# A mixture-of-experts kernel: the exponentials of the fourth routing batch on VectorE as a series instead of ScalarE's table

## The chip, the cores and the metric

The kernel runs on one core of a Trainium2 chip. The metric is the device time of one execution in microseconds (us), as a median over runs. The engines are TensorE (PE in the rows, its weight loads PEld), VectorE (DVE), ScalarE (ACT), GpSimd (POOL) and the DMA queues, which SyncE (SP) and GpSimd start.

## The reference

Input are 8 sequences of 512 rows with 128 features. First comes an LSTM over the 8 sequences (the step runs over the first axis), then a layer norm of x + LSTM(x). Its rows are split into 8 groups of 512 tokens and go through a layer of 8 experts, each token to its best two, with a capacity of 128 tokens for each pair of group and expert. A second layer norm closes.

```python
raw = jax.nn.softmax(logits, axis=-1)          # logits = x @ router_w, 8 experts
idx1 = jnp.argmax(raw, axis=-1)
gate1 = jnp.sum(raw * one_hot(idx1), axis=-1)
rest = raw * (1.0 - one_hot(idx1))
idx2 = jnp.argmax(rest, axis=-1)
gate2 = jnp.sum(rest * one_hot(idx2), axis=-1)
# places in an expert's queue by a cumulative sum, tokens past the capacity are dropped
hidden = gelu(expert_in @ w0) * (expert_in @ w1)
out = combine(hidden @ wo, gate1, gate2)
```

## The kernel before, in words

**First part, the LSTM (0 to about 64 us of the trace).** A loop over the sequences s = 0 to 7 computes the gates with TensorE, activates them on ScalarE (tanh), combines them on VectorE. Among these steps stand the layer norm and the router of the sequences that are done. The router works in four batches b of two groups (8 tiles of 128 tokens each). For a batch, `best` (L938) takes the top values of the logits and writes their distance from the largest into `less`; `scale_less` (L950) multiplies it by the reciprocal deviation; `exp` (L745) on ScalarE writes `ex`, the exponentials, 128 partitions by 64 values; the five steps of `gate_step` (L958) on VectorE sum, divide and choose; `assign_batch` computes each token's slot; GpSimd's `scatter` writes the rows into the experts' slots in DRAM, 16 indirect transfers per batch (L479). The scatters of the four batches stand one behind the other in GpSimd's queue.

**Second part, the experts.** 24 units u, each one expert with two or four groups of slots, are run in a written order. SyncE loads a unit's rows (`load_xd`, L407, into `xd`) once the batches that feed it are scattered. TensorE turns them (`turn_xd`, L594, into `b_xt`), ScalarE and VectorE split the turned rows into a high and a low half (`x_hi` L791, `x_lo` L1082). A unit has 6 chunks k = 0 to 5. For each chunk TensorE computes two products in `first` (L645 to L647, three matmuls each, from the high and low halves of rows and weights; the last chunk has one product). ScalarE applies the gelu (L834, tile `act_g`), VectorE multiplies by the second product (`chunk`, L1116, into one of four buffers called `term_f`, `term_i`, `cell`, `h`), ScalarE makes the high half of the result (L797, `hid_hi` or `h_hi`), VectorE the low half one chunk later (L1090, `hid_lo` or `h_lo`), and TensorE uses both in `second` (L661, L662, L664; for the last chunk L667, L668), three chunks behind `first`. After a unit its output is turned (`turn_y`, L681) and `give` (L1106, L1108) weights it and hands it to GpSimd, which adds it into the tokens in DRAM (L494).

**Around the change.** The first exponential of this part belongs to batch 2 and stands ahead of unit 0. The exponential of the last batch (NB - 1 = 3) stands on ScalarE in unit 1, chunk 4, after the copy of unit 0's output (L803) and the high half of unit 2's rows (L791) and ahead of the gelu of that chunk. The function table that ScalarE holds at that point has the gelu, so the compiled program loads another for the exponential and the gelu's again after it (two `ACT_TABLE_LOAD`). On VectorE `scale_less(3)` stands after chunk 2 of unit 1 and the first step of `gate_step(3)`, which reads `ex`, after chunk 0 of unit 2. The engines' programs run in the order in which they are written; an instruction that waits for a semaphore holds all behind it on its engine.

```python
elif (u, k) == (1, 4):            # ScalarE
    exp(NB - 1)
...
scale_less(NB - 1)                # VectorE
low_weights(2, 3)
for k in range(3, NCH):
    chunk(1, k)
for k in range(NCH):
    chunk(2, k)
    if k < 3:
        for n in range(2 * k, min(2 * k + 2, 5)):
            gate_step(NB - 1, n)
```

## Time and profile before

| | |
|---|---|
| runs, us | 346.48, 347.69, 651.17; median 347.69 |
| profiled execution, its own time | only its span is given |
| span of the profiled execution, us | 342.1 |
| median less span, us | 5.6 |
| busy, share of the span | TensorE 86%, VectorE 74%, ScalarE 64%, GpSimd 55% |
| instructions in the span | 5646 |

The span runs from the first to the last instruction of one execution; a run's time has the start and the end around it. The profile's page gives each engine's busy time, slices of the span, and a chain of waits followed back from the end. A timeline lists instructions with their start, their duration, the engine, the line and the tiles, and in brackets how long the engine was idle before and what it waited for. TensorE's matmuls are pipelined: the starts of its records follow each other more closely than their durations, and the ends are modelled.

### The profile page before, as it was taken

To read this page: it belongs to the slowest core of one execution; us is meant where nothing else is said; L and a number is where in the kernel's file an instruction comes from. 1 tells how busy PE (TensorE), PEld (TensorE's weight loads), DVE (VectorE), ACT (ScalarE), POOL (GpSimd) and SP (SyncE) were. 2 spreads that over 40 slices of the span, in tenths; PEclk is the share of its full clock that TensorE was granted. 3 is DMA by queue.
4 is the path that set the end of the run, shared out by engine and by line. 5 is a ranking of instruction groups with operands and counts; after the bars stand their busy time and mean duration, and the time that the engine had idled before them with its cause. 6 is when DMAs were issued, how large, how long until landed. Compare 5 with 4: busy or idle time off the path is not lost.

```text
span 342.1 us, 5646 instructions
## 1 busy us (share of the span) xinstructions
PE 293.1 (86%) x1692; PEld 244.8 (72%) x1692; DVE 251.6 (74%) x794; ACT 217.3 (64%) x495; POOL 186.6 (55%) x153
## 2 busy tenths in 40 slices
PE   8999999697754695529999999999999999998880
PEld 6666665496744695419999987877888888888770
DVE  2789989599621585026888889889877776996985
ACT  4689887665720473026777876877765566566884
POOL 5012788887777027787773433437436536559500
PEclk9999999999885598557999999999999999999996
DMA  6996582486521015324443326344214227325265
GB/s 218 363 407 167 127 251 74 99 229 191 166 89 57 22 28 151 97 35 47 49 62 57 52 46 175 76 113 64 47 16 63 33 19 134 65 36 86 24 163 153
DMA packets 46685, 37.20 MB, mean 109 GB/s; under 512 B 7057, under 2 KB 40784, under 8 KB 46656
## 3 DMA queue, kind: packets, MB, share of 16 engines
q1 hardware_dynamic: 35392, 26.56, 26.1%
q0 software_dynamic: 11264, 10.29, 19.6%
q8 instruction: 14, 0.23, 0.3%
q14 instruction: 15, 0.12, 0.1%
HBM read 17.86 MB, written 17.10 MB: 102 GB/s over the span
## 4 chain that ended last, share of the span: by engine, by line
PE 67%; DVE 10%; issue 7%; ACT 6%; another core or an unknown queue 5%; POOL 3%; DMA 1%; SPq 0%; ACTq 0%; DVEq 0%
PE big L647 11%; PE big L645 11%; PE big L646 10%; PE big L552 6%; PE b_ht L664 3%; PE b_xnt L661 2%; PE b_xnt L664 2%; PE b_xnt L662 2%; PE b_ht L661 2%; PE b_ht L662 2%; PE big L538 2%; POOL tokens L494 2%; PE b_rt L681 2%; PE big L539 2%
## 5 line engine op out<-in xcount | busy, mean ns | idle before, releaser
L834 ACT ACTIVATE act_g<-big 128x256 f32<-128x256 f32 (+1 forms) x144 | 65.0, 452 | 90.8 <-PE big L647 59.6
L645 PE MATMUL big<-x_hi,e_hi 128*128 128x256 f32 (+1 forms) x264 | 89.5, 339 | 0.3 <-issue 0.3
L647 PE MATMUL big<-x_lo,e_hi 128*128 128x256 f32 (+1 forms) x264 | 86.9, 329 | 1.3 <-issue 1.3
L646 PE MATMUL big<-x_hi,e_lo 128*128 128x256 f32 (+1 forms) x264 | 86.9, 329 | 1.0 <-issue 1.0
L479 POOL DMA_INDIRECT slots<-rows,slot_ix x64 | 68.5, 1071 | 33.6 <-issue 18.5
L494 POOL DMA_INDIRECT tokens<-contrib,token_ix x32 | 51.4, 1607 | 42.2 <-DVE token_ix L1108 34.4
L494 POOL DMA_INDIRECT tokens<-zero_rows,token_ix x28 | 45.2, 1614 | 35.5 <-DVE token_ix L1108 27.5
L646 PEld LDWEIGHTS big<-x_hi,e_lo 128*128 128x128 f32 x264 | 52.9, 200 | 4.5 <-issue 1.1
L647 PEld LDWEIGHTS big<-x_lo,e_hi 128*128 128x128 f32 x264 | 52.7, 199 | 4.4 <-issue 0.4
L645 PEld LDWEIGHTS big<-x_hi,e_hi 128*128 128x128 f32 x264 | 53.0, 201 | 3.7 <-issue 0.2
L1116 DVE TENSOR_TENSOR term_i<-act_g,big 128x256 f32<-128x256 f32 (+3 forms) x36 | 18.3, 508 | 17.4 <-ACT act_g L834 12.0
L1116 DVE TENSOR_TENSOR term_f<-act_g,big 128x256 f32<-128x256 f32 (+1 forms) x36 | 18.3, 508 | 17.2 <-remote 12.9
L1116 DVE TENSOR_TENSOR cell<-act_g,big 128x256 f32<-128x256 f32 (+1 forms) x36 | 18.3, 509 | 14.1 <-ACT act_g L834 8.9
L1116 DVE TENSOR_TENSOR h<-act_g,big 128x256 f32<-128x256 f32 (+3 forms) x36 | 18.3, 508 | 13.6 <-PE big L647 6.5
L762 ACT ACTIVATE act_g<-big,bias_g 128x512 f32<-128x512 f32 x31 | 21.2, 687 | 9.0 <-PE big L552 6.4
L552 PE MATMUL big<-h,u_half 128*128 128x512 f32 x56 | 25.5, 598 | 0.2 <-DVE h L1062 0.2
L460 POOL TENSOR_TENSOR root_y<-root_x,minus_half 128x4 f32<-128x4 f32 x8 | 9.7, 1216 | 25.5 <-DVE root_x L929 25.5
L661 PE MATMUL b_xnt<-hid_hi,e_hi 128*128 128x256 f32 (+1 forms) x48 | 17.2, 358 | 3.7 <-ACT hid_hi L797 1.9
L738 ACT ACTIVATE e_hi<-e_raw 128x544 fp32r<-128x544 f32 x32 | 20.4, 650 | 0.0
L661 PE MATMUL b_ht<-hid_hi,e_hi 128*128 128x256 f32 (+1 forms) x48 | 16.8, 349 | 3.0 <-issue 1.7
L797 ACT ACTIVATE hid_hi<-cell 128x256 fp32r<-128x256 f32 (+1 forms) x36 | 17.3, 482 | 2.9 <-DVE cell L1116 2.1
L664 PE MATMUL b_ht<-hid_lo,e_hi 128*128 128x256 f32 (+1 forms) x48 | 16.5, 344 | 3.1 <-DVE hid_lo L1090 2.0
(204 smaller groups left out, 672.9 us busy)
## 6 DMA issues: line engine op xcount, KB each, us to landing
e_raw<-in_L_ffn_w_kernel_dram SPq DMA_DIRECT2D x16, 320.0 KB
slots<-zero_rows SPq DMA_DIRECT2D x8, 548.0 KB, 7.6
e_raw<-in_L_ffn_wo_kernel_dram SPq DMA_DIRECT2D x8, 320.0 KB
xd<-slots SPq DMA_DIRECT2D x16, 137.0 KB
xd<-slots SPq DMA_DIRECT2D x8, 274.0 KB
e_lo<-e_raw POOLq DMA_DIRECT2D x4, 544.0 KB
x<-in_L_attn_input_seq_dram SPq DMA_DIRECT2D x8, 256.0 KB, 4.5
tokens<-rows SPq DMA_DIRECT2D x8, 256.0 KB
```

The costliest lines, as they stand in the source:

```text
L479: pool.indirect_dma_start(slots, bass.IndirectOffsetOnAxis(ap=slot_ix[b][:, 2 * t + c:2 * t + c + 1], axis=0), rows[:, b * BT + t, :], Non ...
L494: pool.indirect_dma_start(tokens, bass.IndirectOffsetOnAxis(ap=tokens_of(u)[:, k:k + 1], axis=0), contrib(u)[:, k, :], None, bounds_check= ...
L552: pe.matmul(big[k][:, :], u_half[:, g * D:(g + 1) * D], h2[:, :], start=False, stop=True).then_inc(gate_ready, 1)
L645: pe.matmul(dst, e_hi[q][:, c0:c0 + m], xdt_hi[u % 2][:, 0:w], start=True, stop=False)
L646: pe.matmul(dst, e_lo[q][:, c0:c0 + m], xdt_hi[u % 2][:, 0:w], start=False, stop=False)
L647: mm = pe.matmul(dst, e_hi[q][:, c0:c0 + m], xdt_lo[u % 2][:, 0:w], start=False, stop=True)
L661: pe.matmul(y, hi, hid_hi[r][:, 0:w], start=(k == 0), stop=False)
L664: mm = pe.matmul(y, hi, hid_lo[r][:, 0:w], start=False, stop=False)
L738: nc.scalar.activation(e_hi[e % RING_E][:, piece(n)], e_raw[e % 2][:, piece(n)], ACT.Copy).then_inc(ehi_ready[e % RING_E], 1)
L762: nc.scalar.activation(act_g[k][:, :], big[k][:, :], ACT.Tanh, bias=bias_g[:, gate_order[k]:gate_order[k] + 1], scale=1.0 if k == 2 else 0 ...
L834: nc.scalar.activation(act0[n % RH][0:m, 0:w], pre(n, P)[0], ACT.Gelu_apprx_tanh).then_inc(gelu_ready, 1)
L1116: dve.tensor_tensor(hid[n % RH][0:m, 0:w], act0[n % RH][0:m, 0:w], pre(n, P)[1], ALU.mult).then_inc(hid_ready, 1)
```

## The change

The call of `exp` for the last batch leaves ScalarE. In its place VectorE computes the same 128 by 64 exponentials in 14 steps (15 instructions), all in float32: the argument is cut off at -87, divided by ln 2 and rounded (by adding and taking away 1.5 * 2^23), the rest is formed with ln 2 in two parts, the power of two is put together as an integer, and a polynomial of degree seven is evaluated by Horner's rule; values under -87 become 0. Each step but one instruction waits for the step before it by a semaphore of its own, `exp_step`. The steps stand ahead of the last three chunks of unit 1: four, five and five. Batches 0, 1 and 2 keep ScalarE's exponential. Five work tiles are added, 128 by 64 each.

```diff
--- before.py
+++ after.py
@@ -9,6 +9,7 @@
 
 
 
+import math
 from contextlib import ExitStack
 
 import concourse.bass as bass
@@ -70,6 +71,11 @@
     AS = 6
     RH = 4
 
+    SERIES = [1.0 / math.factorial(n) for n in range(7, 0, -1)]
+    EXP_STEPS = 7 + len(SERIES)
+    EXP_LOW, LOG2E, ROUND = -87.0, 1.4426950408889634, 1.5 * (1 << 23)
+    LN2_HIGH, LN2_LOW = 0.693359375, -2.12194440054690e-4
+
     gate_order = [1, 0, 3, 2]
 
     with ExitStack() as ctx:
@@ -130,6 +136,9 @@
         top_ix = sb("top_ix", [P, BT, E], U32)
         less, ex = sb("less", [P, BT, E]), sb("ex", [P, BT, E])
         total, rtotal = sb("total", [P, BT]), sb("rtotal", [P, BT])
+        ex_x, ex_n = sb("ex_x", [P, BT * E]), sb("ex_n", [P, BT * E])
+        ex_r, ex_q = sb("ex_r", [P, BT * E]), sb("ex_q", [P, BT * E])
+        ex_two = sb("ex_two", [P, BT * E], I32)
         gates = sb("gates", [P, BT, 2])
         choice = sb("choice", [P, BT, 2])
         chosen = sb("chosen", [P, BT, 2, E], BF16)
@@ -197,6 +206,7 @@
         var_ready, power_ready, root_ready = sem("var_ready"), sem("power_ready"), sem("root_ready")
         xn_ready = sem("xn_ready")
         logits_ready, scaled, exp_ready = sem("logits_ready"), sem("scaled"), sem("exp_ready")
+        exp_step = sem("exp_step")
         top_ready, less_ready, topix_ready, gates_step = sem("top_ready"), sem("less_ready"), sem("topix_ready"), sem("gates_step")
         base_step = sem("base_step")
         chosen_ready, places_ready, slot_step = sem("chosen_ready"), sem("places_ready"), sem("slot_step")
@@ -822,8 +832,6 @@
                         norm_rows(S - 2, range((k - 1) * T // 2, k * T // 2))
                     elif (u, k) in ((0, 4), (0, 5)):
                         norm_rows(S - 1, range((k - 4) * T // 2, (k - 3) * T // 2))
-                    elif (u, k) == (1, 4):
-                        exp(NB - 1)
                     n = u * NCH + k
                     m = P if k < FULL else P // 2
                     if n >= RH:
@@ -954,6 +962,35 @@
                 dve.wait_ge(power_ready, GB * (b + 1))
                 view = less[:, :, :].rearrange("p (g t) e -> p g t e", g=GB)
                 dve.tensor_tensor(view, view, root_y[:, :, 0:T].unsqueeze(3).broadcast_to([P, GB, T, E]), ALU.mult).then_inc(scaled, 1)
+
+            def exp_by_series(n):
+
+                x, out = less[:, :, :].rearrange("p t e -> p (t e)"), ex[:, :, :].rearrange("p t e -> p (t e)")
+                if n:
+                    dve.wait_ge(exp_step, n)
+                else:
+                    dve.wait_ge(scaled, NB)
+                if n == 0:
+                    ins = dve.tensor_scalar(ex_x[:, :], x, EXP_LOW, None, ALU.max)
+                elif n == 1:
+                    ins = dve.tensor_scalar(ex_n[:, :], ex_x[:, :], LOG2E, ROUND, ALU.mult, ALU.add)
+                elif n == 2:
+                    ins = dve.tensor_scalar(ex_n[:, :], ex_n[:, :], -ROUND, None, ALU.add)
+                elif n == 3:
+                    ins = dve.scalar_tensor_tensor(out=ex_r[:, :], in0=ex_n[:, :], scalar=-LN2_HIGH, in1=ex_x[:, :], op0=ALU.mult, op1=ALU.add)
+                elif n == 4:
+                    dve.tensor_scalar(ex_two[:, :], ex_n[:, :], 127.0, float(1 << 23), ALU.add, ALU.mult)
+                    ins = dve.scalar_tensor_tensor(out=ex_r[:, :], in0=ex_n[:, :], scalar=-LN2_LOW, in1=ex_r[:, :], op0=ALU.mult, op1=ALU.add)
+                elif n == 5:
+                    ins = dve.tensor_scalar(ex_q[:, :], ex_r[:, :], SERIES[0], None, ALU.mult)
+                elif n < 5 + len(SERIES):
+                    ins = dve.scalar_tensor_tensor(out=ex_q[:, :], in0=ex_q[:, :], scalar=SERIES[n - 5], in1=ex_r[:, :], op0=ALU.add, op1=ALU.mult)
+                elif n == 5 + len(SERIES):
+                    ins = dve.scalar_tensor_tensor(out=ex_q[:, :], in0=ex_q[:, :], scalar=1.0, in1=ex_two[:, :].bitcast(F32), op0=ALU.add, op1=ALU.mult)
+                else:
+                    dve.scalar_tensor_tensor(out=out, in0=x, scalar=EXP_LOW, in1=ex_q[:, :], op0=ALU.is_ge, op1=ALU.mult).then_inc(exp_ready, 1)
+                    return
+                ins.then_inc(exp_step, 1)
 
             def gate_step(b, n):
 
@@ -1210,6 +1247,8 @@
             scale_less(NB - 1)
             low_weights(2, 3)
             for k in range(3, NCH):
+                for n in range(EXP_STEPS * (k - 3) // 3, EXP_STEPS * (k - 2) // 3):
+                    exp_by_series(n)
                 chunk(1, k)
             for k in range(NCH):
                 chunk(2, k)
```

On ScalarE in unit 1, from the copy of unit 0's output on, before the change (`tanh_c` is the tile of that copy, `act_g` the gelu's output, `hid_hi<-term_i` the high half of chunk 3):

```order
L803 ACTIVATE tanh_c<-b_ht 128x256
L791 ACTIVATE x_hi<-b_xt 128x256
L747 ACT_TABLE_LOAD
L747 ACTIVATE ex<-less 128x64
L834 ACT_TABLE_LOAD
L834 ACTIVATE act_g<-big 128x256
L797 ACTIVATE hid_hi<-term_i 128x256
```

and after it:

```order
L813 ACTIVATE tanh_c<-b_ht 128x256
L801 ACTIVATE x_hi<-b_xt 128x256
L842 ACTIVATE act_g<-big 128x256
L807 ACTIVATE hid_hi<-term_i 128x256
L842 ACTIVATE act_g<-big 64x256
```

The two table loads and the exponential are gone; the gelu of chunk 4 follows the high half of unit 2's rows directly.

On VectorE in unit 1, from the low half of a piece of expert 2's weights (`e_lo`) over chunks 3 and 4 up to chunk 5 (`term_i`, `cell` and `h` are the outputs of chunks 3, 4 and 5, `x_lo` the low half of unit 2's rows), before the change:

```order
L1027 TENSOR_TENSOR e_lo<-e_raw,e_hi 128x544
L1116 TENSOR_TENSOR term_i<-act_g,big 128x256
L1090 TENSOR_TENSOR hid_lo<-term_f,hid_hi 128x256
L1082 TENSOR_TENSOR x_lo<-b_xt,x_hi 128x256
L1116 TENSOR_TENSOR cell<-act_g,big 128x256
L1090 TENSOR_TENSOR hid_lo<-term_i,hid_hi 128x256
L1116 TENSOR_TENSOR h<-act_g,big 64x256
```

and after it, up to the last step ahead of chunk 4:

```order
L1064 TENSOR_TENSOR e_lo<-e_raw,e_hi 128x544
L974 TENSOR_SCALAR ex_x<-less 128x64
L976 TENSOR_SCALAR ex_n<-ex_x 128x64
L978 TENSOR_SCALAR ex_n<-ex_n 128x64
L980 SCALAR_TENSOR_TENSOR ex_r<-ex_n,ex_x 128x64
L1153 TENSOR_TENSOR term_i<-act_g,big 128x256
L1127 TENSOR_TENSOR hid_lo<-term_f,hid_hi 128x256
L1119 TENSOR_TENSOR x_lo<-b_xt,x_hi 128x256
L982 TENSOR_SCALAR ex_two<-ex_n 128x64
L983 SCALAR_TENSOR_TENSOR ex_r<-ex_n,ex_r 128x64
L985 TENSOR_SCALAR ex_q<-ex_r 128x64
L987 SCALAR_TENSOR_TENSOR ex_q<-ex_q,ex_r 128x64 x3
```

Four instructions of the series came in ahead of chunk 3 and of everything behind it, `x_lo` among it, and six ahead of chunk 4.

On VectorE from chunk 4 of unit 1 on, after the change:

```order
L1153 TENSOR_TENSOR cell<-act_g,big 128x256
L1127 TENSOR_TENSOR hid_lo<-term_i,hid_hi 128x256
L987 SCALAR_TENSOR_TENSOR ex_q<-ex_q,ex_r 128x64 x3
L989 SCALAR_TENSOR_TENSOR ex_q<-ex_q,ex_two 128x64
L991 SCALAR_TENSOR_TENSOR ex<-less,ex_q 128x64
L1153 TENSOR_TENSOR h<-act_g,big 64x256
```

Five more instructions came in ahead of chunk 5. No instruction of TensorE, GpSimd or SyncE moved.

## Rows read from the trace of the kernel before

**Rows 1.** The page, part 1: busy time of each engine.
```profile
PE 293.1 (86%) x1692; PEld 244.8 (72%) x1692; DVE 251.6 (74%) x794; ACT 217.3 (64%) x495; POOL 186.6 (55%) x153
```

**Rows 2.** Stretches: length, busy us (instructions) per engine, granted clock, DMA, GB/s.
```profile
88.00:92.00 4.00, 2.19 (x11) 1.98 (x10) 2.17 (x7) 3.30 (x8) 3.19 (x3) 0.77 0.81 259
92.00:96.00 4.00, 3.56 (x25) 3.36 (x24) 2.03 (x8) 0.88 (x3) 3.09 (x4) 0.81 0.43 123
96.00:118.00 22.00, 11.12 (x57) 9.36 (x57) 6.58 (x25) 5.56 (x17) 11.86 (x13) 0.60 0.15 47
130.00:155.00 25.00, 10.52 (x52) 9.00 (x51) 5.70 (x15) 4.48 (x14) 19.27 (x18) 0.59 0.41 95
155.00:180.00 25.00, 25.00 (x202) 25.00 (x202) 20.80 (x58) 17.37 (x53) 18.52 (x12) 0.93 0.43 53
```

**Rows 3.** Timeline of TensorE: start, us, engine, line, op, tiles, idle before.
```profile
86.92 0.28 PE L664 MATMUL b_xnt<-hid_lo,e_hi 128*128 128x256 f32 x1
...
87.08 0.41 PE L681 MATMUL b_xt<-ident,tanh_c 128*128 128x128 f32 x2
...
88.01 0.28 PE L647 MATMUL big<-x_lo,e_hi 128*128 128x256 f32 x1
...
90.09 0.57 PE L661 MATMUL b_xnt<-hid_hi,e_hi 128*128 128x256 f32 x1 [1.81 <-issue]
...
94.72 0.28 PE L647 MATMUL big<-x_lo,e_hi 128*128 128x256 f32 x1
...
95.44 0.44 PE L594 MATMUL b_xt<-ident,xd 128*128 128x128 f32 x2 [0.44 <-DMA xd<-slots]
...
95.95 0.29 PE L664 MATMUL b_ht<-hid_lo,e_hi 128*128 128x256 f32 x1
```

**Rows 4.** Timeline of ScalarE around the fourth exponential.
```profile
86.49 1.28 ACT L747 ACT_TABLE_LOAD   x1
87.78 0.26 ACT L747 ACTIVATE ex<-less 128x64 f32<-128x64 f32 x1
88.06 1.28 ACT L834 ACT_TABLE_LOAD   x1
89.35 0.38 ACT L834 ACTIVATE act_g<-big 128x256 f32<-128x256 f32 x1
89.63 0.41 ACT L797 ACTIVATE hid_hi<-term_i 128x256 fp32r<-128x256 f32 x1
```

**Rows 5.** Timeline of VectorE in the same stretch.
```profile
85.67 0.42 DVE L1116 TENSOR_TENSOR term_i<-act_g,big 128x256 f32<-128x256 f32 x1
...
86.51 0.43 DVE L1082 TENSOR_TENSOR x_lo<-b_xt,x_hi 128x256 fp32r<-128x256 f32 x1
...
89.77 0.42 DVE L1116 TENSOR_TENSOR cell<-act_g,big 128x256 f32<-128x256 f32 x1 [2.84 <-ACT act_g L834]
...
90.11 0.42 DVE L1090 TENSOR_TENSOR hid_lo<-term_i,hid_hi 128x256 fp32r<-128x256 f32 x1
...
90.56 0.42 DVE L1116 TENSOR_TENSOR h<-act_g,big 64x256 f32<-64x256 f32 x1
...
93.57 0.42 DVE L1090 TENSOR_TENSOR hid_lo<-term_f,hid_hi 128x256 fp32r<-128x256 f32 x1
```

**Rows 6.** Groups of VectorE by form: busy us, mean ns.
```profile
L956 DVE TENSOR_TENSOR less<-less,root_y 128x64 f32<-128x64 f32 x4 | 0.9, 219 | 0.0
```

**Rows 7.** Timeline of VectorE, two dependent steps of an earlier batch's softmax.
```profile
31.22 0.20 DVE L966 RECIPROCAL rtotal<-total 128x8 f32<-128x8 f32 x1
31.45 0.17 DVE L969 TENSOR_TENSOR gates<-ex,rtotal 128x16 f32<-128x16 f32 x1
```

**Rows 8.** Timeline of GpSimd's queue, the last scatter of batch 1.
```profile
89.48 0.98 POOL L479 DMA_INDIRECT slots<-rows,slot_ix  x1 [0.30 <-issue]
```

**Rows 9.** Timeline of SyncE's queue, the loads of unit inputs behind it.
```profile
92.97 38.19 SPq L407 DMA_DIRECT2D xd<-slots  x5
```

**Rows 10.** Timeline of ScalarE after 95 us.
```profile
108.66 0.38 ACT L834 ACTIVATE act_g<-big 128x256 f32<-128x256 f32 x1 [6.78 <-remote]
```

## The prediction, made before the changed kernel ran

> **What bounds the kernel now.** I read the busy times first: TensorE is busy 293.1 us of 342.1, more than any other engine [rows 1], so ScalarE's time counts only where TensorE waits for it. The windows then show where TensorE is not full: it is busy 2.19 us of the 4 from 88 to 92, 11.12 of 22 from 96 to 118 and 10.52 of 25 from 130 to 155, and full from 155 to 180 [rows 2]. The first of these holes lies on the edit. TensorE's timeline shows a matmul at 88.01 and the next at 90.09, the first of chunk 3's second product; where TensorE is full a matmul follows the one before it in 25 / 202 = 0.12 us [rows 2], so 2.08 less 0.12 = 1.96 us are lost [rows 3]. The bracket says only "issue", but ScalarE's timeline gives the cause: table load at 86.49, exponential at 87.78, table load at 88.06, gelu at 89.35, and only then, at 89.63, the high half of chunk 3, done at 90.04 [rows 4]. The granted clock of 88 to 92 is 0.77 and of 92 to 96 is 0.81 [rows 2]: together (0.23 + 0.19) x 4 x 2 = 3.4 us at the lower level, 1.2 GHz, right behind that wait; work that takes 3.4 us there takes 1.7 at 2.4 GHz. So the wait costs 2.0 us and up to 1.7 more.
>
> The question is what comes next. At 95.44 TensorE turns the rows of unit 3, after waiting 0.44 us for the DMA that brings them [rows 3]. Its last matmul ahead of that starts at 94.72 and ends at 95.00, so the rows were there at about 95.4, and TensorE was early. These rows are group 2 and 3's slots: SyncE issues their load at 92.97 [rows 9], once batch 1's scatter has landed, whose last issue starts on GpSimd at 89.48 in a queue that has idled only 0.30 us between issues [rows 8]. Neither queue has an instruction that the edit moves, and this scatter waits for nothing that ScalarE or VectorE do in unit 1.
>
> **ScalarE's side.** Removed: 1.28 + 0.26 + 1.28 us and the small gaps between, 86.49 to 89.35 = 2.86 us [rows 4]. Without it the gelu of chunk 4 starts at 86.49, the high half of chunk 3 at 86.77 and is done at 87.18, before TensorE asks for it at 88.13 or later. The wait for ScalarE is gone entirely; what is late next is VectorE.
>
> A rule of the Trainium skill says more: "ScalarE: Activation LUTs", section "What ACT_TABLE_LOAD costs", puts a switch at 1283 ns for the load and about 1380 ns for a drain. By that two switches would cost 5.3 us, and the edit would free 5.6 us of ScalarE. The trace agrees with the load (1.28) and shows no drain: both loads, the exponential and all gaps fit into 2.86 us [rows 4]. I go by the trace.
>
> **VectorE's side.** 15 instructions of 128x64 float32 come in. The nearest form is `scale_less`, also 128x64: 219 ns [rows 6]. From one dependent step to the next there is little: the reciprocal starts at 31.22, takes 0.20, and the step that waits for it by a semaphore starts at 31.45, 0.03 later [rows 7]. So 0.25 us for a dependent step; one of the 15 doesn't wait for the one before and costs about 0.14. The sum is 14 x 0.25 + 0.14 = 3.6 us: 1.0 ahead of chunk 3, 1.4 ahead of chunk 4, 1.25 ahead of chunk 5. The 0.14 is the 0.22 less an overlap of 0.08, which instructions that don't wait for each other show: one at 89.77 takes 0.42, the next starts at 90.11 [rows 5]. Bounds for a step: 0.14 for every step would make 2.1 us for all; 0.42, what an instruction with four times as many elements takes [rows 5], would make 6.3. I take 0.25, since the form is the same as that of [rows 6].
>
> Walked through: chunk 3 starts at 85.67 + 1.0 = 86.7 and `x_lo`, two instructions of 0.34 later, at 87.35, done at 87.8 where it was done at 86.94 [rows 5]. The turning of unit 0's output waits for it and moves from 87.08 to about 87.85; the products of unit 2's chunk 0 behind it, whose last matmul starts 0.93 later at 88.01 [rows 3], are started by 88.8 instead of 88.0, and TensorE is free at 88.9. The second batch of steps ends at 89.1; chunk 4, which waited for the gelu until 89.77 [rows 5], starts then, and chunk 3's low half is done at 89.9. TensorE needs it for the third matmul from there, at 89.15, so it waits 0.75 us where it waited 2.0. The third batch of steps ends at 91.0, where chunk 5 starts, 0.5 later than its 90.56. From there to the end of the instruction at 93.57 VectorE ran without a longer break in 3.4 us [rows 5]; now it is done at 94.4 and not 94.0. In all VectorE, which had idled 2.84 us ahead of 89.77 [rows 5], fills that gap with the series and comes out 0.4 us later. The instruction at 93.57 makes the low half that TensorE uses at 95.95 [rows 3]: slack of 1.5 us left. TensorE itself, held twice by VectorE (low halves of chunks 4 and 5), comes to the turning of unit 3 at about 94.2, 0.8 us before it did, and then waits for the same DMA until 95.44.
>
> **Sum.** Saved up to 95 us: 2.0 of waiting and up to 1.7 of clock, less about 2.9 us of new waits for VectorE's low halves, in all 0.8. Given back at 95.44: 0.8. From there every engine has the same work in the same order, with three instructions fewer on ScalarE, long past; the first reader of `ex` on VectorE stands behind unit 2's chunk 0, the series is done before chunk 5 of unit 1, by 91.0, so the routing of batch 3 isn't later. The span stays at 342.1 less at most a few tenths. With the 5.6 us around it (median 347.69 less span 342.1) that is 347.7; I take 0.4 off, for what a warmer clock at 95 may give, and say 347.3.
>
> **Rivals.** (a) The gain is carried on. For it: from 96 on the engines wait for things that the trace doesn't name (ScalarE is idle 6.78 us ahead of the gelu at 108.66, "remote" [rows 10]); if TensorE's results already come late at 95, the edge at 95.44 is softer than it reads, and work ahead of it counts. Against it: the bracket names the DMA. Time: at most 2.0 + 1.7 = 3.7 us off, 344.0.
>
> (b) The hole of 96 to 118 belongs to the first. It holds 57 matmuls in 22 us, and 155 to 180 holds 202 in 25 [rows 2]; at that rate 57 take 7.1, so 15 us are lost there, and I can't name what holds the results. If TensorE's pause of 2 us and its lowered clock set it off, it goes with them: 347.7 - 15 - 2 = 331. Against it: the like hole of 130 to 155 has no table load ahead of it.
>
> (c) VectorE becomes the bound and the kernel is slower. From the numbers above a step may cost 1.5 / 15 = 0.10 us more, 0.35, before the low half for 95.95 is late. At 0.6 us a step, if the semaphore's round trip or the conversion to an integer costs so much, it is 15 x 0.25 = 3.75 late, with a pause that keeps the clock low for 3.4 us more (1.7): 353.1.
>
> (d) The two long holes are sensitive to small shifts and one more appears or one grows: 15 us, 363.
>
> (e) The edit doesn't do what it says: the compiled order shows no table load left in unit 1, so I give this nothing.
>
> **How the numbers follow.** Forecast 0.62, (a) 0.17, (b) 0.09, (c) 0.08, (d) 0.04. The forecast's own range is 346 to 348.5, the spread of the undisturbed runs shown. For 8 in 10 the range takes in (a), nearly all of (c), and some growth or shrinkage of the holes by a third; (b) and (d) stay out: 341.5 to 351.5. A change of over 2% (7 us) is about what a measurement of this kernel can tell from none. Faster by that: (b) and a part of a shrinking hole, 0.10. Slower: (d) and a tail of (c), 0.06. Within: 0.84.
>
> **What would show it.** Right: no table load between 86 and 90, ScalarE's gelu of chunk 4 near 86.5; VectorE busy through 87 to 90 with 15 instructions at 0.25 us; no gap of TensorE over 1 us before 95; the turning of unit 3 again at about 95.4, now after a longer wait for the DMA (over 1 us); the span within 1 us. Wrong: that turning clearly before 95 or with no wait, which is (a); 96 to 118 with over 100 matmuls, which is (b); steps of over 0.35 us and the low half behind 96, which is (c).

## The result, and the profile after

Changed kernel: median 348.82 us of 20 runs (345.26 to 707.34). Kernel before, beside it on the same chip: median 347.19 us of 20 runs (345.30 to 651.17). The ratio on record is 1.0098, 95% interval [1.0056, 1.0139]: 1% slower, where the forecast was 0.1% faster. A ratio is formed from each kernel's fast runs, those within 1.5% of its fastest, and so needn't be the quotient of the medians beside it, which are of all runs. The 1.0098 can't be rebuilt from the 20 runs of each kernel: the medians give 1.0047, and the means without the three runs over 400 us give 1.0035, give or take 0.0042, which doesn't exclude 1.

One thing is needed to read all that follows: the runs went to several chips. The first comparison ran at a level of about 348 us, as chip 11 has it later; on three other chips (15, 3 and 1) the kernel before takes 306 us, with the same instructions. I call them the slower chip and the faster chips.

The page of the kernel after, its span and part 1:

```profile
span 348.5 us, 5658 instructions
PE 293.6 (84%) x1692; PEld 245.2 (70%) x1692; DVE 254.3 (73%) x809; ACT 215.0 (62%) x492; POOL 185.7 (53%) x153
```

Against [rows 1]: VectorE has 15 instructions and 2.7 us more, ScalarE three instructions and 2.3 us less, TensorE nearly the same. The run of this profile took 350.68 us, so 2.2 us lie around the span. I had set 5.6 for it, because for the kernel before I had only its span and the median of other runs. Its profiled run lay at 342.1 + 2.2 = 344.3 us, below every run listed for it: an unusually fast one.

The windows after, in the stretches of [rows 2] (without 118 to 130) and two ahead of them (length, busy us and instructions of TensorE, its weight loads, VectorE, ScalarE and GpSimd, granted clock, DMA share, GB/s):

```profile
80.00:84.00 4.00, 2.90 (x21) 2.50 (x21) 3.90 (x21) 1.05 (x3) 3.08 (x4) 1.00 1.02 306
84.00:88.00 4.00, 1.44 (x9) 1.26 (x8) 0.85 (x3) 0.68 (x2) 3.08 (x4) 0.72 0.20 67
88.00:92.00 4.00, 2.77 (x14) 2.39 (x13) 0.76 (x2) 0.69 (x2) 3.08 (x4) 0.50 0.19 63
92.00:96.00 4.00, 2.76 (x11) 2.17 (x10) 2.24 (x8) 0.69 (x2) 3.08 (x4) 0.50 0.19 46
96.00:118.00 22.00, 6.31 (x26) 5.75 (x27) 5.68 (x22) 3.67 (x12) 11.69 (x12) 0.50 0.30 94
130.00:155.00 25.00, 14.31 (x97) 12.86 (x95) 10.41 (x31) 7.95 (x23) 16.97 (x17) 0.78 0.35 99
155.00:180.00 25.00, 21.21 (x158) 20.91 (x159) 17.22 (x48) 14.96 (x45) 20.09 (x14) 0.81 0.42 48
```

The slow stretch that began at about 94 us before begins at about 81 us after: from 84 to 88 TensorE has 9 matmuls where the kernel before had 35:

```profile
84.00:88.00 4.00, 4.00 (x35) 3.88 (x34) 2.85 (x8) 3.17 (x8) 3.29 (x3) 1.00 0.40 110
```

ScalarE's gelus show what an engine sees inside the stretch:

```profile
80.65 0.38 ACT L842 ACTIVATE act_g<-big 64x256 f32<-64x256 f32 x1 [0.39 <-PE big L657]
...
85.65 0.38 ACT L842 ACTIVATE act_g<-big 128x256 f32<-128x256 f32 x1 [4.04 <-PE big L657]
...
89.96 0.38 ACT L842 ACTIVATE act_g<-big 128x256 f32<-128x256 f32 x1 [3.62 <-PE big L657]
...
113.96 0.38 ACT L842 ACTIVATE act_g<-big 128x256 f32<-128x256 f32 x1 [10.20 <-remote]
...
114.54 0.36 ACT L842 ACTIVATE act_g<-big 64x256 f32<-64x256 f32 x1
...
115.15 0.37 ACT L842 ACTIVATE act_g<-big 128x256 f32<-128x256 f32 x1
```

The gelus start 3 to 13 us apart and wait for TensorE's product, though TensorE itself is idle 5.0 of the 12 us from 84 to 96 (12 less 1.44, 2.77 and 2.76): the products reach the others late. The gelu at 85.65 starts 1.1 us behind the modelled end of its product's last matmul (84.25 + 0.28), the one at 89.96 starts 0.8 behind; in a trace of the same kernel on a faster chip each gelu from 85 to 112 us that waited for TensorE starts 0.1 behind. The gelu at 85.65 belongs to unit 1's chunk 0, three chunks ahead of the first series step. So in this profile the stretch begins ahead of the edit, and it can't be the edit's work that sets it off. The series' own steps stand at 94.70 and later here, among instructions that wait for the stretch. The prediction's signs can't be read in this profile: the gelu of unit 1's chunk 4, forecast for 86.5, is the one at 113.96, and unit 3's rows are turned at 120.2.

The stretch ends at the same time in both traces, at about 114 us, but with less done. The gelu at 115.15 is unit 2's first; the kernel before has unit 3's first there:

```profile
114.89 0.36 ACT L834 ACTIVATE act_g<-big 128x256 f32<-128x256 f32 x1
```

The changed kernel is one unit behind, and it stays so: unit 7's first gelu starts at 170.1 and not at 163.8, 6.3 us later, as much as the next unit takes in either trace. The spans differ by 6.4 us.

### The profile page after: what moved, and what is told of

Its sections match the earlier page's. It is cut to its first block, busy times and chain, and to the rows that moved or that the text cites. A ratio compares the mean times of both kernels' runs of the same rounds, so it can differ in the third digit from the quotient of the medians.

```text
span 348.5 us, 5658 instructions
## 1 busy us (share of the span) xinstructions
PE 293.6 (84%) x1692; PEld 245.2 (70%) x1692; DVE 254.3 (73%) x809; ACT 215.0 (62%) x492; POOL 185.7 (53%) x153
## 4 chain that ended last, share of the span: by engine, by line
PE 68%; issue 10%; DVE 9%; another core or an unknown queue 5%; ACT 5%; POOL 3%; ACTq 0%; DVEq 0%; POOLq 0%
PE big L657 11%; PE big L655 10%; PE big L656 10%; PE big L562 6%; PE b_ht L674 3%; PE b_xnt L671 3%; PE b_xnt L674 2%; PE b_xnt L672 2%; PE b_ht L671 2%; PE b_ht L672 2%; PE big L548 2%; POOL tokens L504 2%; PE b_rt L691 2%; PE big L550 2%
## 5 line engine op out<-in xcount | busy, mean ns | idle before, releaser
L489 POOL DMA_INDIRECT slots<-rows,slot_ix x64 | 67.2, 1050 | 41.6 <-DVE slot_ix L1053 22.1
L671 PEld LDWEIGHTS b_xnt<-hid_hi,e_hi 128*128 128x128 f32 x48 | 9.9, 205 | 20.9 <-issue 11.4
L807 ACT ACTIVATE h_hi<-h 128x256 fp32r<-128x256 f32 (+3 forms) x36 | 17.4, 482 | 1.9 <-DVE h L1153 1.5
```

The source lines that it names most:

```text
L489: pool.indirect_dma_start(slots, bass.IndirectOffsetOnAxis(ap=slot_ix[b][:, 2 * t + c:2 * t + c + 1], axis=0), rows[:, b * BT + t, :], Non ...
L671: pe.matmul(y, hi, hid_hi[r][:, 0:w], start=(k == 0), stop=False)
```

## The experiments

Four theories. **A**: the series costs more than the table loads gave. **B**: the edit gives and takes nothing; where the late stretches begin decides the 1%, and that is chance. **C**: a longer pause of TensorE lowers its clock behind it, so a gain ahead of it is turned into a loss. **D**: batch 2's and 3's scatters hold TensorE's results back. Later **F**, the forecast's own step: what is gained ahead is given back at the turning of unit 3's rows. The runs came in five jobs, each with its own runs of the kernel before on the same chip; every ratio is to those.

### On the slower chip: unaltered, removed, both, placed behind

The first changes nothing. The second leaves out the fourth batch's exponential (its gates come from batch 2's), so it has neither table loads nor series:

```diff
-                    elif (u, k) == (1, 4):
-                        exp(NB - 1)
-                    dve.wait_ge(exp_ready, b + 1)
+                    dve.wait_ge(exp_ready, min(b, NB - 2) + 1)
```

The third is the changed kernel with ScalarE's exponential put back and the series written to a tile that nobody reads. The fourth puts each batch of series steps behind the chunk instead of ahead of it.

> The changed kernel once more, unaltered, for a second interval and a second trace. Theory A (the edit costs: VectorE's 15 instructions make TensorE late by more than the two table loads gave): again 1.005 to 1.014 of the kernel before. Theory B (nothing is lost or won by the edit, and what differs is how long the two stretches last in which TensorE's results come late, before unit 6): the ratio comes out at 1.000 to 1.005, and the trace has the stretches at other places or of other lengths than the first trace, with units 6 to 23 equal to the tenth of a us.

> The fourth exponential is left out on ScalarE and no series is put in: batch 3's gates are formed from the exponentials of batch 2, which still stand in ex. The removal alone. Theory A: the removal saves what it frees up to the wait for unit 3's rows, 0.990 to 0.998. Theory B and my forecast's step at 95.44: 0.998 to 1.002, since TensorE only comes earlier to a DMA that GpSimd's queue times. Theory C (the pause for the table loads is useful, because the late stretches follow dense work of TensorE): slower, 1.004 to 1.012, although work is only taken away.

> Both: ScalarE's exponential with its two table loads stays and gives the result, and VectorE computes the series beside it into a tile that nobody reads. The addition alone. Theory A: slower, 1.004 to 1.012. Theory B: 1.000 to 1.004, VectorE idles 2.8 us there anyway. Theory C: 0.998 to 1.003, since the pause is back.

> The changed kernel with each group of series steps behind its chunk instead of ahead of it, so that chunks 3, 4 and 5 of unit 1 and the low halves come 1.0 to 1.4 us earlier and only what follows them is held. Theory A (the low halves held by the series are the cost): most of the loss goes, 0.998 to 1.004. Theory B: as e1_again within 0.3%. Theory C: as e1_again or slower.

| | median us (runs) | lowest, highest | ratio, 95% interval |
|---|---|---|---|
| before | 349.36 (11) | 346.18, 353.10 | |
| unaltered | 348.46 (6) | 346.37, 351.02 | 1.0004 [0.9942, 1.0066] |
| removed | 345.48 (6) | 341.38, 348.86 | 0.9871 [0.9806, 0.9936] |
| both | 350.88 (6) | 345.47, 350.98 | 0.9963 [0.9874, 1.0053] |
| behind | 349.23 (6) | 345.97, 350.74 | 1.0013 [0.9956, 1.0070] |

The 1.0% didn't come back with the same kernel, though the two intervals overlap. The kernel with both costs says little: four of its six runs lie at 350.9 to 351.0, and only the other two enter its ratio, so its ratio is under 1 while its median is the highest of the five. The removal's 1.3% speaks for A, which had expected 0.2 to 1.0%. It was not measured alone on this chip again; on the faster chips below it comes out slower than before. The windows from 84 to 92 show what moves the time. Unaltered (span 348.8 us) and behind (span 343.8 us), with the same 15 steps:

```profile
84.00:88.00 4.00, 1.09 (x7) 0.88 (x7) 1.31 (x4) 0.68 (x2) 3.08 (x4) 1.00 0.21 69
88.00:92.00 4.00, 2.47 (x10) 2.10 (x10) 0.40 (x1) 0.00 (x0) 3.09 (x4) 0.56 0.15 51
```

```profile
84.00:88.00 4.00, 3.30 (x24) 2.69 (x23) 2.41 (x7) 1.74 (x7) 3.09 (x4) 1.00 0.20 69
88.00:92.00 4.00, 2.05 (x11) 1.45 (x11) 1.68 (x7) 0.60 (x3) 3.08 (x4) 1.00 0.71 202
```

In the first the stretch is there from 84, in the second from about 87. Unit 0's first gelu, ahead of all that the edit touches, starts at 74.9 in the first and at 72.0 in the second (73.7 in the profile after, 71.8 in that before). A late unit 0 doesn't bring an early stretch by itself, though: in two later traces of this chip, with the turning one chunk later (below), unit 0 starts at 73.1 (changed) and 74.6 (before), the stretch begins at about 88 and 90, and the spans are 345.6 and 344.6.

### On a faster chip: with more matmuls that keep TensorE warm

Meant for the slower chip, to see if a warmer clock at unit 0 sets where the stretch begins:

```diff
-            keep_warm(8, big[2])
+            keep_warm(16, big[2])
             turn_xd(0)
+            keep_warm(4, big[2])
```

for the kernel before, the changed one and the removal. The fourth, for D, lets batches 2 and 3 scatter only each token's first choice (half of their transfers; the second choice's rows are left out).

> The kernel before with 12 more idle matmuls around the turning of unit 0's rows (8 ahead of it, 4 behind), where TensorE waits 2 and 1 us. The traces so far fall into two kinds: in two of six TensorE's clock falls at 68 us, unit 0 starts its gelus at 73.7 or later instead of 71.8, and its results come late from 81 us on instead of 87 to 94; both have spans of 348.5 and 348.8 against 342 to 344. Theory B (the two kinds make the spread, whatever the edit): the high values near 350 get rare, 0.990 to 0.996 of the kernel before, and the trace has the clock at 1.0 from 60 to 85. If the kinds come from elsewhere: 0.998 to 1.006.

> The changed kernel with the same 12 idle matmuls, so that the edit is compared with less spread, against e5_warm_before. Theory A (the series costs more than the table loads): 0.5 to 1.4% above e5. Theory B (the edit moves nothing): within 0.4% of e5.

> The kernel before without the fourth exponential (batch 3's gates from the exponentials of batch 2) and with the same 12 idle matmuls: the removal alone, a second time. If e2_drop_exp's 0.987 is the removal's own gain: 0.8 to 1.5% below e5. If it was the draw of the runs: within 0.4% of e5. Theory C (the pause is useful): above e5.

> The kernel before, in which batches 2 and 3 scatter only the rows of the first choice: 8 transfers each in GpSimd's queue instead of 16, so 10.3 us less per batch; their second choices are left out of the result. The late results of TensorE ended in all six traces between 113 and 115 us, right behind the end of batch 2's scatter (last issue 109.4 to 110.5). Theory D (the scatters hold TensorE's results back, from some backlog on until they end): the first stretch ends near 103 and the second is some 10 us shorter, and the span falls by 10 to 20 us, 0.94 to 0.97. If the stretches don't hang on the scatters: they end where they did and the time is 0.995 to 1.005.

The kernel before took 306.12 us here (29 runs, 304.86 to 307.06), 41 us less, and no trace has a late stretch. Warmed before 306.56, 1.0043 [1.0015, 1.0072]; warmed after 307.30, 1.0033 [1.0010, 1.0056]; warmed removal 308.85, 1.0079 [1.0054, 1.0104]; half scatter 305.95, 0.9988 [0.9974, 1.0001]. So the edit is worth nothing here (1.0033 beside 1.0043), the removal alone costs 0.4% more than either, and D can't be tested where there is no stretch; the scatters bound nothing here. Why less work doesn't take less time shows in TensorE's timeline at the turning of unit 3's rows. Warmed before:

```profile
88.30 0.39 PE L662 MATMUL b_xnt<-hid_hi,e_hi 128*128 128x256 f32 x1 [1.69 <-ACT hid_hi L798]
...
93.12 0.28 PE L648 MATMUL big<-x_lo,e_hi 128*128 128x256 f32 x1
95.13 0.44 PE L594 MATMUL b_xt<-ident,xd 128*128 128x128 f32 x2 [1.73 <-DMA xd<-slots]
```

Warmed after:

```profile
86.46 0.39 PE L675 MATMUL b_xnt<-hid_lo,e_hi 128*128 128x256 f32 x1 [0.19 <-DVE hid_lo L1128]
...
88.81 0.38 PE L675 MATMUL b_xnt<-hid_lo,e_hi 128*128 128x256 f32 x1 [0.51 <-DVE hid_lo L1128]
...
90.77 0.39 PE L675 MATMUL b_xnt<-hid_lo,e_hi 128*128 128x256 f32 x1 [0.63 <-DVE hid_lo L1128]
...
92.16 0.36 PE L678 MATMUL b_xnt<-h_hi,e_lo 128*128 128x256 f32 x1 [0.30 <-DVE h_hi L1128]
...
93.07 0.28 PE L658 MATMUL big<-x_lo,e_hi 128*128 128x256 f32 x1
95.66 0.44 PE L604 MATMUL b_xt<-ident,xd 128*128 128x128 f32 x2 [2.32 <-DMA xd<-slots]
```

Warmed removal:

```profile
89.94 0.28 PE L648 MATMUL big<-x_lo,e_hi 128*128 128x256 f32 x1
96.08 0.69 PE L594 MATMUL b_xt<-ident,xd 128*128 128x128 f32 x2 [5.86 <-DMA xd<-slots]
```

One wait of 1.69 us for ScalarE is replaced by four for VectorE's low halves, 1.63 us in all, and all three end at the same DMA at 95 to 96 us, whenever they arrive. The removal arrives 3 us earlier and waits 5.86. The granted clock of 88 to 92 and of 92 to 96 is 0.68 and 0.89 in the warmed kernel before and 1.00 and 1.00 in the warmed changed one; in the removal it is 0.74 from 92 to 96 and 0.50 from 96 to 100.

### On another faster chip: plain, removed, filled, doubled

The changed kernel and the removal again without warming. The third puts matmuls of ones ahead of the wait, in the bank that the turning fills:

```diff
             def turn_xd(u):
+                if u == 3:
+                    pe.wait_ge(contrib_ready, 2 * min(u - 2, GB + 1))
+                    keep_warm(24, b_xd(u))
                 pe.wait_ge(xd_in[u % 4], 16 * (u // 4 + 1))
```

The fourth sets a further instruction of the same size ahead of each dependent step of the series:

```diff
-                    dve.wait_ge(exp_step, n)
+                    dve.wait_ge(exp_step, 2 * n)
...
+                dve.scalar_tensor_tensor(out=ex_s[:, :], in0=(ex_q if n > 5 else ex_x)[:, :] if n else x, scalar=1.0, in1=x, op0=ALU.add, op1=ALU.mult).then_inc(exp_step, 1)
+                dve.wait_ge(exp_step, 2 * n + 1)
```

> The changed kernel unaltered, once more. The two chips seen so far gave 349 and 306 us for the kernel before, and the long stretches in which TensorE's results come late stood only in the slower. The last three traces of the faster one show the edit at work: with the series TensorE waits 0.19, 0.51 and 0.63 us for low halves in unit 1 and 2, and comes to the turning of unit 3's rows at 93.3, where it waits 2.32 us for the DMA; without exponential and series it comes at 90.2 and waits 5.86. Theory F (the forecast: what is gained ahead is given back at this DMA): the time is that of before within 0.3%, on either chip: 306 +-1 at the faster. Theory A (the series costs more than the table loads gave): over 1.005, 308 or more. Theory B (the 1.0% measured belongs to the stretches of the slower chip, where a few tenths of a us decide how long they last): at the faster chip 1.000 +-0.003, at the slower anything within 1.5% of before.

> Leaves out the fourth batch's exponential altogether (the gates come from an older batch's, so the outputs differ), without the warming matmuls of the last run. Theory F with theory C (the pause is given back at the DMA, and a pause of over 5 us there lowers the clock of the 9 us that follow): 0 to 1% slower than before, 306 to 309 at the faster chip, with the granted clock under 0.8 right behind the turning of unit 3's rows. Theory A: 1% faster than before, 303. The difference to the changed kernel in the same job is the series' own price: under A +5 us, under F zero or below.

> As the run before it, and 24 matmuls of ones by ones are put ahead of TensorE's wait for unit 3's rows, into the bank that the turning then fills. They take 24 x 0.2 = some 5 us of a pause of 5.9 and delay nothing else. If the lowered clock behind that pause is what makes the removal slower (C), the time falls below that of the run without them by 1 to 3 us, to before's or just under (305 to 306 at the faster chip), and the granted clock stays at 1.00 from 92 to 106. If the pause's place and not the clock costs the time, it equals the run without them.

> The changed kernel with each dependent step of the series preceded by one more of the same size that writes to a tile that nobody reads and that the step waits for: 14 instructions more, 14 x 0.25 = 3.5 us more of VectorE ahead of chunks 3, 4 and 5 of unit 1. Theory A (the series stands on the path): the time grows by all of it, 3.5 us over the changed kernel. Theory F: the wait for unit 3's rows was 2.3 us at the faster chip and takes that much of it; the time grows by 3.5 - 2.3 = 1.2 us and up to 1 more by the clock, as TensorE's waits ahead of it grow to 1 us and more each. If it grows by nothing, the low halves of unit 2 have more slack than I read.

| | median us (runs) | ratio, 95% interval |
|---|---|---|
| before | 306.56 (23) | |
| changed, unaltered | 306.69 (12) | 1.0005 [0.9985, 1.0025] |
| removed | 308.35 (12) | 1.0050 [1.0022, 1.0077] |
| removed, filled with 24 | 308.25 (6) | 1.0058 [1.0037, 1.0080] |
| doubled | 310.80 (5) | 1.0133 [1.0112, 1.0154] |

The first agrees with the forecast's ratio (347.3 / 347.69 = 0.999) within 0.2%. VectorE's timeline of that run has the whole series (start, us, engine, line, op, tiles):

```profile
86.24 0.19 DVE L974 TENSOR_SCALAR ex_x<-less 128x64 f32<-128x64 f32 x1
86.46 0.20 DVE L976 TENSOR_SCALAR ex_n<-ex_x 128x64 f32<-128x64 f32 x1
86.69 0.20 DVE L978 TENSOR_SCALAR ex_n<-ex_n 128x64 f32<-128x64 f32 x1
86.92 0.23 DVE L980 SCALAR_TENSOR_TENSOR ex_r<-ex_n,ex_x 128x64 f32<-128x64 f32 x1
87.07 0.42 DVE L1153 TENSOR_TENSOR term_i<-act_g,big 128x256 f32<-128x256 f32 x1
...
88.06 0.19 DVE L982 TENSOR_SCALAR ex_two<-ex_n 128x64 int32<-128x64 f32 x1
88.16 0.22 DVE L983 SCALAR_TENSOR_TENSOR ex_r<-ex_n,ex_r 128x64 f32<-128x64 f32 x1
88.42 0.27 DVE L985 TENSOR_SCALAR ex_q<-ex_r 128x64 f32<-128x64 f32 x1
88.72 0.77 DVE L987 SCALAR_TENSOR_TENSOR ex_q<-ex_q,ex_r 128x64 f32<-128x64 f32 x3
89.41 0.41 DVE L1153 TENSOR_TENSOR cell<-act_g,big 128x256 f32<-128x256 f32 x1
...
90.07 0.73 DVE L987 SCALAR_TENSOR_TENSOR ex_q<-ex_q,ex_r 128x64 f32<-128x64 f32 x3
90.84 0.23 DVE L989 SCALAR_TENSOR_TENSOR ex_q<-ex_q,ex_two 128x64 f32<-128x64 f32 x1
91.10 0.23 DVE L991 SCALAR_TENSOR_TENSOR ex<-less,ex_q 128x64 f32<-128x64 f32 x1
91.36 0.42 DVE L1153 TENSOR_TENSOR h<-act_g,big 64x256 f32<-64x256 f32 x1
```

Dependent steps follow each other in 0.22 to 0.30 us, and the conversion to an integer (`ex_two`) is no dearer. The three batches take 87.07 - 86.24 = 0.83, 89.41 - 88.06 = 1.35 and 91.36 - 90.07 = 1.29, in all 3.5 us.

For C, the windows from 92 to 100 of the removal and then of the filled one:

```profile
92.00:96.00 4.00, 0.56 (x3) 0.56 (x4) 0.87 (x4) 0.58 (x3) 3.04 (x4) 0.95 0.49 136
96.00:100.00 4.00, 4.00 (x31) 3.99 (x31) 2.14 (x8) 1.76 (x5) 3.13 (x3) 0.62 0.18 57
```

```profile
92.00:96.00 4.00, 4.00 (x38) 4.00 (x38) 1.06 (x4) 0.83 (x3) 3.08 (x4) 1.00 0.57 148
96.00:100.00 4.00, 4.00 (x45) 3.99 (x44) 1.63 (x7) 1.76 (x5) 3.08 (x4) 1.00 0.15 49
```

Unfilled, the turning starts at 95.44 after 3.91 us of waiting, the clock of the next 4 us is 0.62, and unit 3's first gelu follows at 100.9, 5.5 us behind. Filled, the clock stays at 1.00 and the gelu follows 3.8 us behind the turning, as in the changed kernel (94.59, 98.5). So behind the turning the lower clock costs 1.6 us. But the filling itself took 5.52 us and ended at 96.97, 1.5 us after the rows had come in the unfilled run. In its own run they came sooner still: their load was issued at 91.64 and not at 93.03, and in other traces a turning that waits starts 2.2 to 3.1 us behind that issue, so by estimate they were there at 93.8 to 94.7, and the filling took some 2.3 to 3.1 us in place of the clock's 1.6. I had expected a gain and got none; the likely reason is that I had sized the filling by the longest wait seen. That taking the low clock away shortens the time is thus argued from these traces and shown by no run.

The doubled series costs 310.80 - 306.69 = 4.1 us for 14 added steps of 0.25 (3.5). I expected 1.2 to 2.2 under F, from a wait of 2.3 us at the turning that should have taken part of it, and the whole 3.5 under A. A's figure came out: in the run of the changed kernel in this job that wait is zero (the turning at 94.59 follows its neighbour at once), so nothing was there to take the added steps. The 15 steps of the edit cost nothing beside the table loads (1.0005), but steps beyond them do. TensorE's waits for low halves are 1.28, 1.77 and 1.79 us, and the clock of 96 to 100 is 0.50.

### The turning one chunk later

If the wait for unit 3's rows is where the gain ends, then moving it must free it. On all three engines:

```diff
-                    if k == 3 and u + 1 < NU:
+                    if k == (4 if u == 2 else 3) and u + 1 < NU:
                         turn_xd(u + 1)
```

for the removal, the changed kernel and the kernel before, beside the removal filled with 16 matmuls.

> The last filled run kept the clock at 1.00 but was no faster than the unfilled one: its filling took 5.52 us from 91.61 and ended at 97.0, when the rows had been there since 95.4 in the unfilled trace. So it paid 1.5 us in place where it saved the clock. Now 16 matmuls of ones in place of 24, 16 x 0.23 = 3.7 us, which end at about 95.3. Theory C (the removal of the exponential is slower because the longer pause lowers the clock behind it): 1.5 us less than with 24 and than without any, 306.8, at most 0.1% over before. If the clock behind the pause isn't what costs, it stays at 308.

> Exponential left out, and the turning of unit 3's rows (with its two copies on ScalarE and VectorE) comes one chunk later, behind chunk 4 of unit 2. Theory F (the gain ends at this turning's wait): a chunk of TensorE's work, some 1.1 us, moves ahead of the wait, which falls from 3.9 to 2.8; the time falls by 1.1 us and up to 1 more by the clock, to 306.5 +-0.8. If the gain is lost elsewhere, it stays at 308.3.

> The changed kernel with that turning one chunk later. Of two traces one had no wait there and one 2.3 us. Theory F: 0 to 1.1 us less, 306.0, ratio 0.998 +-0.003 to before. If the two copies moved with it come late for unit 3's chunk 0, it is slower by up to 1 us.

> The kernel before with that turning one chunk later. Its trace with warming matmuls had 1.73 us of wait there. Theory F: 1.1 us less, 305.4, ratio 0.996 +-0.003; a version that is a little faster than both, if it holds. If the wait isn't on the path to the end, 1.000.

This job fell on the slower chip, where before took 347.68 us (23 runs, 343.13 to 353.93). Filled with 16: 352.38, 1.0159 [1.0007, 1.0311]. Removal: 348.58, 1.0069 [1.0018, 1.0120]. Changed: 347.71, 1.0028 [0.9975, 1.0082]. Before: 350.72, 1.0131 [1.0020, 1.0242]. The first ratio rests on two of its six runs. Read alone, the last one says that a turning one chunk later costs 1.3%; none of the four tells C or F. So two of them were run again, and that job went to a faster chip:

> The four kernels of the last job ran on a chip of the slower kind, where before itself ranged from 343 to 354 us, and ratios of 1.003 to 1.016 came out for edits of about a us. So this is once more the kernel without the exponential and with the turning of unit 3's rows one chunk later, for a chip of the faster kind, where it means something: there the removal with the turning in its place was 1.005 [1.0022, 1.0077]. Theory F: 306.5 +-0.8, a ratio of 1.000 +-0.003. If the gain is lost elsewhere, 308.3 again. On the slower kind it tells nothing beyond its spread of 1.5%.

> Once more the kernel before with that turning one chunk later. Theory F at the faster kind of chip: 305.4, ratio 0.996 +-0.003; 1.000 if that wait isn't on the path to the end. On the slower kind theory B (a few tenths of a us decide how long the long stretches last) lets it come out anywhere within 1.5% of before, and not again at 1.013 in particular.

Before took 306.48 us (23 runs). The removal with the later turning: 306.64 (12 runs), 1.0019 [0.9997, 1.0041]. The kernel before with it: 306.08 (12 runs), 0.9994 [0.9977, 1.0011]. The same edit that measured +1.3% on the slower chip measures nothing. For the removal, the later turning takes the ratio from 1.0050 to 1.0019, about 1 us, as F expected; but the intervals ([1.0022, 1.0077] and [0.9997, 1.0041]) overlap, and the two are from different chips. TensorE's timeline of that run, at the turning:

```profile
93.90 0.44 PE L594 MATMUL b_xt<-ident,xd 128*128 128x128 f32 x2 [2.92 <-DMA xd<-slots]
```

and its windows from 92 to 100:

```profile
92.00:96.00 4.00, 2.10 (x24) 1.95 (x25) 1.40 (x6) 1.07 (x3) 3.06 (x4) 1.00 0.46 123
96.00:100.00 4.00, 4.00 (x37) 4.00 (x36) 3.49 (x13) 2.50 (x7) 3.13 (x3) 1.00 0.29 88
```

The wait is 2.92 us, the clock stays at 1.00, and the span is 302.2, the shortest seen. This execution is the fastest of its 12 (304.40 us, median 306.64), and its rows came 1.5 us sooner than in the unfilled removal's trace (93.90 and 95.44). Wait and clock changed together here, so the run doesn't tell C from F. For the kernel before with the later turning F expected 0.996, and that missed (0.9994): only 0.39 us of wait are left at 95.17, and the time didn't fall. Either the 1.73 us of the warmed trace are not there without the warming matmuls, or that wait isn't on the path to the end; the runs don't say which. No version that computes the right result was measurably faster than both kernels.

## Why the prediction was right or wrong

**ScalarE's 2.86 us: right.** The table loads are gone, and on a faster chip the kernel before (here with the later turning) shows them as in [rows 4]:

```profile
86.25 1.28 ACT L747 ACT_TABLE_LOAD   x1
87.54 0.26 ACT L747 ACTIVATE ex<-less 128x64 f32<-128x64 f32 x1
87.82 1.28 ACT L834 ACT_TABLE_LOAD   x1
89.11 0.38 ACT L834 ACTIVATE act_g<-big 128x256 f32<-128x256 f32 x1
```

89.11 - 86.25 = 2.86 again. That the Trainium skill ("ScalarE: Activation LUTs", section "What ACT_TABLE_LOAD costs") adds a drain of about 1380 ns to each switch is borne out by none of these rows; going by the trace was right.

**The series' price: right.** Forecast 0.25 us a step and 3.6 in all; measured 0.22 to 0.30 and 3.5. Rival (c) stayed away at 15 steps. Twice the steps brought it about, with 4.1 us.

**0.8 us gained ahead of 95: right in sum, wrong in parts.** Unit 0's first gelu starts at 70.3 in the warmed kernel before and at 71.0 in the warmed changed one; TensorE's last matmul ahead of the turning ends at 93.40 and 93.35. From the one to the other that is 23.1 and 22.4 us, so 0.7 gained. The new waits are 1.63 us and not the 2.9 that I set against 3.7 saved. The wait saved is 1.69 us, and the lower clock of the warmed kernel before ((0.32 + 0.11) x 4 us) is worth at most 1.7 more; less the new waits that would be 1.8 gained, and 0.7 were. So two terms were too large, the new waits and the clock's part, and that their difference came out is luck. In a kernel with the same wait of 1.67 us for ScalarE (before, with the later turning, on a faster chip) the clock is 1.00 all the way from 80 to 140.

**Given back at the turning: borne out by one pair of traces, where the chip is undisturbed.** Between the warmed kernels the wait grows from 1.73 to 2.32 us, and their times agree (1.0043 and 1.0033). In the plain changed kernel there is no wait at that turning, though the prediction named one of over 1 us as a sign: the load of the rows was issued at 91.60 there and TensorE came at 94.59. Its time is that of before all the same (1.0005), and there is no trace of the plain kernel before on a faster chip to set beside it. The runs add what I had not priced: with the exponential only taken out, TensorE arrives so early that it waits 3.91 and 5.86 us, the clock behind is 0.62 and 0.50, and the kernel with less to do becomes 0.5% slower. The clock accounts for 1.6 us behind the turning in the traces (C), and the kernel with the later turning, in which both wait and clock are better, is about 1 us faster (F). How much of the 0.5% is either's is not shown.

**The measured 1.0%: the step that failed is "from there every engine has the same work in the same order", so "the span stays at 342.1 less at most a few tenths".** It takes the late stretches of 96 to 118 and 130 to 155 as fixed. They are not: the first one's beginning lay at 81 and 84 us in two profiles of the changed kernel, at 87 with its steps placed behind, and at 94 before, and the spans are 348.5, 348.8, 343.8 and 342.1. In the profile after, that is one unit less done by 115 us, 6.3 us. The own range of 346 to 348.5 was taken from the two undisturbed of three runs and too narrow; the runs of either kernel go from 345.3 to 353, leaving out the three over 400. Rival (d) had the right place, with 15 us for a jump instead of the 5 to 6 between these spans, and a chance of 0.04. Rival (b) was right that these stretches don't belong to the kernel's needs (without them it takes 306 us), and wrong in that TensorE's pause at the table loads sets them off: they stay without any exponential.

**What stays open.** Whether the 1.0% is the edit's. For B speak: a repeat with 1.0004 [0.9942, 1.0066]; the stretch that begins ahead of the edit in the profile; the lowest and, without the three over 400, the highest runs of both kernels alike (345.30 and 353.27, 345.26 and 353.10); and the share of runs above 349 us, which is much the same at this level: 21 of 52 for the kernel before (5 of 18, 6 of 11 and 10 of 23 in three jobs) and 11 of 25 for the changed one (8 of 19 and 3 of 6), leaving out the same three. That this chip gives 1.0131 for an edit that measures 0.9994 on a faster one may be chance or the stretches. Against B, the interval on record of the first comparison excludes 1 (its listed runs don't, see the result), it and the repeat's overlap between 1.0056 and 1.0066, the profile before has the latest beginning of the stretch of all, and whether the edit shifts the odds of an early stretch there was not settled. It is shown only that on faster chips the edit costs nothing, series included.

## What to carry to other kernels

Work taken off ahead of a wait for a DMA is worth nothing until that wait is gone, and can cost: in the traces the longer pause lowered TensorE's clock for the next microseconds (1.6 us here). Look for the next wait that doesn't depend on the edit, and move it or what it waits for first. Before a difference of 1% is believed, run the same comparison again, on another chip if there is one: here one kernel took 348 us on one and 306 on three, and on the slower one ratios from 0.987 to 1.016 came out for edits of a kind that moved the time by 0.6% at most on the faster ones.

## What was not expected of the hardware

- One program takes 306 us on three chips and 348 on a fourth, with equal parts elsewhere: from unit 7's first gelu to unit 23's it takes 156.4 to 157.3 us on the slower and 156.4 to 156.6 on the others. The 41 us lie in two stretches in which TensorE's products reach the other engines late and gelus start up to 13 us apart. The first ends about 4 us behind batch 2's last scatter issue (109.2 to 110.5 us, the stretch's end at 113 to 115), the second 6 to 9 us behind batch 3's. On the faster chips the same scatters run and nothing is late. What delays the products isn't shown.
- Unit 0 starts at 70.3 to 71.0 us in some executions on the faster chips and at 72.7 to 73.8 in others, and where TensorE waits for the rows of unit 3 they come at 93.9 to 96.1 either way: this wait evens out early and late executions.
- TensorE's granted clock fell behind waits of 3.91 and 5.86 us for unit 3's rows and not behind ones of 2.32 and 2.92; a pause of 1.67 us for ScalarE left it at 1.00 in one trace, and one of 1.69 us was followed by 0.68 in the window of 88 to 92 in another.
